# Last expert stage of a decoder: the small places of the second table mixed among the full ones

## The reference, cut to what matters

```python
h = silu(einsum('td,ehd->teh', xf, w1))          # 8 experts, 256 -> 512
expert_out = einsum('teh,edh->ted', h, w2)        # 512 -> 256
out = einsum('te,ted->td', comb, expert_out)      # comb is zero but for two experts of a token
x = x + out
```

## Time and profile before

| | us |
|---|---|
| median of 3 runs | 3156.68 |
| lowest and highest | 3152.07, 3157.47 |
| the profiled execution | 3149.4 |
| its span, first to last instruction | 3147.6 |
| mean granted clock of TensorE, share of full speed | 0.949 |

### The profile page before, as it was taken

One profiled execution on the slowest core, in us unless ns is written; L12 is line 12 of the kernel. 1 busy time (PEld: TensorE's weight loads), 2 busy tenths in 40 slices (PEclk: granted clock), 3 DMA queues, 4 the chain that ended last, 5 costly groups with the idle time before them and its releaser, 6 DMA issues.

```text
span 3147.6 us, 49455 instructions
## 1 busy us (share of the span) xinstructions
PE 2695.4 (86%) x16576; PEld 1841.3 (58%) x16576; DVE 1900.7 (60%) x3513; ACT 1524.2 (48%) x2641; POOL 1498.4 (48%) x1619
## 2 busy tenths in 40 slices
PE   5888888876888888878999999899888888868996
PEld 2333333323555566645688887697455555557885
DVE  3788888784787678863222222501688988883211
ACT  4565666543776666631122221444666666643332
POOL 3577666673545567634322222200345555543443
PEclk8999999988999999989999999899999999978998
DMA  9700000001005000002377775200000100006875
GB/s 326 240 0 1 0 1 1 1 0 38 20 16 189 1 1 0 1 22 89 104 217 207 210 211 156 71 1 1 1 16 31 37 33 31 22 20 193 231 216 155
DMA packets 137956, 244.75 MB, mean 78 GB/s; under 512 B 15936, under 2 KB 111424, under 8 KB 127040
## 3 DMA queue, kind: packets, MB, share of 16 engines
q1 hardware_dynamic: 111168, 207.61, 20.1%
q0 software_dynamic: 26592, 34.63, 5.6%
HBM read 151.28 MB, written 92.73 MB: 78 GB/s over the span
## 4 chain that ended last, share of the span: by engine, by line
PE 34%; DVE 6%; issue 6%; POOL 6%; ACT 2%; DMA 2%; POOLq 0%; DVEq 0%; ACTq 0%
PE PS L2442 11%; PE PS L2398 6%; PE PS L2066 4%; PE PS L2705 3%; PE PS L2718 3%; POOL e_hs L1544 3%; DMA out<-e_dead,f_token 2%; POOL e_qs L1547 1%; DVE e_mx L1447 1%; PE PS L1399 1%; POOL rows_in_place L878 1%; PE PS L2057 1%; DVE e_pr L1451 1%; PE PS L1337 1%; DVE e_den L1458 1%
## 5 line engine op out<-in xcount | busy, mean ns | idle before, releaser
L578 POOL TENSOR_TENSOR u_in<-dtx,b_rep 128x512 f32<-128x512 f32 x256 | 325.1, 1293 | 201.3 <-ACT b_rep L559 200.1
L594 DVE TENSOR_TENSOR_SCAN state<-PS,u_in 128x512 f32<-128x512 f32 x256 | 312.2, 1220 | 59.2 <-POOL u_in L578 34.9
L551 PE MATMUL PS<-scaled,ident 128*128 128x512 f32 x512 | 295.6, 661 | 28.8 <-DVE scaled L588 28.7
L2459 ACT ACTIVATE d_act_b<-PS 128x256 f32<-128x256 f32 (+2 forms) x192 | 76.6, 400 | 447.5 <-PE PS L2442 409.8
L1544 POOL TENSOR_TENSOR e_hs<-e_pr 128x512 f32<-128x512 f32 x128 | 162.9, 1272 | 236.5 <-ACT e_pr L1511 235.1
L1544 POOL TENSOR_TENSOR u_hs<-u_pr 128x512 f32<-128x512 f32 x128 | 166.1, 1298 | 229.1 <-ACT u_pr L1511 228.5
L2442 PE MATMUL PS<-d_unit_T,d_w 128*128 128x256 f32 (+1 forms) x1280 | 260.7, 356 | 1.1 <-ACT d_unit_T L2452 1.1
L2468 DVE TENSOR_TENSOR d_hid<-d_act_b,PS 128x256 f32<-128x256 f32 (+2 forms) x192 | 84.4, 440 | 283.3 <-ACT d_act_b L2459 246.1
L2362 POOL DMA_INDIRECT out_by_token<-d_y_rows,d_token x71 | 110.8, 1561 | 300.3 <-DVE d_y_rows L2489 201.6
L567 ACT ACTIVATE PS<-dt,decay_rate 128x508 f32<-128x508 f32 x256 | 173.5, 687 | 138.0 <-DVE state L594 136.1
L2442 PEld LDWEIGHTS PS<-d_unit_T,d_w 128*128 128x128 f32 x1280 | 221.0, 190 | 26.3 <-DVE d_hid L2468 1.3
(11 more groups left out here) (453 smaller groups left out, 6145.1 us busy)
## 6 DMA issues: line engine op xcount, KB each, us to landing
d_w<-in_d_w SPq DMA_DIRECT2D x42, 1024.0 KB, 6.1
e_dead<-in_f_w SPq DMA_DIRECT2D x40, 1024.0 KB
rows_in_place<-blank SPq DMA_DIRECT2D x136, 272.0 KB, 4.7
d_w<-in_d_w SPq DMA_DIRECT2D x42, 512.0 KB
rows_by_expert<-zeros SPq DMA_DIRECT2D x36, 272.0 KB, 3.6
d_unit_rows<-rows_by_expert SPq DMA_DIRECT2D x31, 272.0 KB
e_dead<-rows_in_place SPq DMA_DIRECT2D x31, 272.0 KB
X<-in_x SPq DMA_DIRECT2D x8, 512.0 KB, 11.7
```

What stands on the lines that cost most here:

```text
L551: nc.tensor.matmul(YB[:, c], ident[:], scaled[:, (KD * n + c) % RC], start=False, stop=n == NS - 1).then_inc(m_y, 1)
L578: nc.gpsimd.tensor_tensor(u_in[:, k % RU], dtx[:, p, c], b_rep[:, n % RB], ALU.mult).then_inc(m_u, 1)
L594: nc.vector.tensor_tensor_scan(state[:, k % 2], DECAY[:, k % RD], u_in[:, k % RU], 0.0, ALU.mult, ALU.add).then_inc(m_h, 1)
```

## The change

In the second table the places take another turn. After the 21 places of the first table come one full place, then nine times a full place and a small one. Before, ten full places came first and then nine small ones. The place numbers of each kind stay in their order, and the last place is the small one with the last number in both. Places 21 and 22 are the same as before; place 23 is now the first small one.

```diff
-    plan = [(2, 2 * n) for n in range(early)] + [(2, 2 * n) for n in range(full)]
-    return early, full, plan + [(1, 2 * full + n) for n in range(single)]
+    plan = [(2, 2 * n) for n in range(early)]
+    pairs, ones = [(2, 2 * n) for n in range(full)], [(1, 2 * full + n) for n in range(single)]
+    alone = max(full - single, 0)
+    plan += pairs[:alone]
+    for n in range(single):
+        plan += pairs[alone + n:alone + n + 1] + ones[n:n + 1]
+    return early, full, plan
```

## The result

The changed kernel is slower: its median is 3168.36 us of 18 runs (3158.98 to 3195.09), the kernel before has 3156.45 us in 18 runs beside it. The ratio is 1.0052 with a 95% interval from 1.0038 to 1.0065, so 12 to 21 us are lost. The forecast was 12 us gained.

What follows compares the result with a forecast made beforehand. The serial scatters bound the end: last output 3122.0, plus 0.14, 0.48 and 0.86, 3.4 lag and 8.7 to the end give span 3135.6, 12.0 us less; median 3156.7 to 3144.7 us, range 3138 to 3155.

Steps and rivals of the forecast that it cites:

- The chain of scatters bounds the end, not PE: End of the span: the last scatter is issued 13.6 us after PE's last output, so the serial scatters end last.
- PE's waits for weights go away, its last output comes 3 us earlier: Small places: three waits of 3.31 us in all taken as 0, PE's end from 3125.3 to 3122.0.
- the sum of the links: Second table: a link is the distance of two places' first scatters; a pair's two links keep pace up to 11.27 us.
- one slip: Nine pairs: only one has both links dear, 16.45 us, 5.2 over the cadence; lag at the last scatter taken as 3.4.
- the dear links (8.55 and 7.90): Profile before: link of full place 30 (8.55 us) and of a small place (7.90), used together for one pair.
- The argument for it was a share: Second table: a full and a small place take the DMA engines 9.1 of PE's 11.27 us, 0.81, leaving room.
- Four places now are 22.5 us of PE's time: DVE, token buffers: four places last 22.5 us and not 15.7, so its 12.7 us of waits for a buffer go.
- Rival 2: Full places' second tile waits behind the small place's weights: full links 8.55, small 5.16, loss 7.8 us; chance 0.08.
- a late chain thins the loads out: Argument against the slower case: a late chain lets PE run only four places ahead, and loads then thin out.
- The Trainium skill's rule on turns between queues: DMA engines: a tile waits behind one packet of a weight load, a full place's two tiles twice; speaks against the change.
- The last places win back 2 us: New places 37 to 39, empty with hardly a load: 9.0 us a pair against PE's 11.27, hiding 2 us of lag.
- The premise of the whole gain: Second table: with full and small places mixed the chain nearly keeps pace; 12.0 us gained, at most 15.4.

Runs made afterwards that it cites:

- e2: Changed kernel with eight token and y buffers, not four: first scatter of place 22 to that of place 39 115.1 us, ratio 1.0001 to the kernel before.
- e15: Changed order, eight token and y buffers, fourth weight buffer, wide POOL memset, but SP doesn't wait for it: places 22 to 39 115.9 us, ratio 1.0035 to before.
- e13: Changed order, eight token and y buffers, fourth weight buffer, loads wait for a wide POOL memset behind the scatters: places 22 to 39 98.2 us, ratio 0.9967 to before.
- e3: Changed kernel with each weight load issued as four of 256 KB: places 22 to 39 126.9 us, ratio 1.0095 to the kernel before.
- e4: Kernel before with each weight load issued as four of 256 KB: places 22 to 39 110.3 us, ratio 1.0031 to the kernel before.
- e1: Changed kernel, but places 24 to 39 load no weights: places 22 to 39 97.0 us, ratio 0.9958 to the kernel before.
- e6: Kernel before, but places 24 to 39 load no weights: places 22 to 39 98.0 us, ratio 0.9962 to the kernel before.
- e14: Kernel before with eight token and y buffers, fourth weight buffer, loads behind scatters by a wide POOL memset: places 22 to 39 99.6 us, ratio 0.9979 to before.
- e8: Changed kernel, eight token and y buffers, three weight buffers, loads wait for a narrow POOL memset behind the scatters: places 22 to 39 143.0 us, ratio 1.0112 to before.
- e10: Changed kernel, eight token and y buffers, four weight buffers, loads wait for a narrow POOL memset behind the scatters: places 22 to 39 107.7 us, ratio 1.0017 to before.
- e12: Changed kernel, but places 24 to 39 load only half the weights (512 KB): places 22 to 39 100.2 us, ratio 0.9960 to the kernel before.

## Why the prediction was wrong, point by point

- *The chain of scatters bounds the end, not PE:* right. Before and after it is what ended last, and all of the loss is in its links.
- *PE's waits for weights go away, its last output comes 3 us earlier:* wrong. Up to place 35 they did, and up to place 34 the loads came 7.0 and 4.5 us apart (7.0 and 4.3 forecast). Behind that PE waited 6.4 us. Counted from the scatter of place 22, its last output ended at 105.9 us and not at 95.3 as before. PE's four waits for weights all lie behind 3110 us, where the lock sets SP's beat, and in e2, without the lock, there is none. So this was a consequence of the late chain.
- *The step that failed is the sum of the links,* "I therefore don't add 1.3 us for each of nine pairs, 11.7 us, but count one slip ... 5.2 us over the cadence, and keeping pace before and after". The six pairs with loads took 97.3 us in place of 67.6: not one slip of 5 us but one in every pair. I had the dear links (8.55 and 7.90) in my rows and took them for exceptions. e15 against e13 shows that they are the rule in this order as long as loads go out in PE's beat. Among the full places of the order before, with one load in 7.35 us, they are not (links of 7.39 us in the mean).
- *The argument for it was a share:* 0.81 of the DMA engines' time being taken, there would be room. The share was 0.83 and didn't decide, as e13 runs a quick chain at 0.82. A serial chain pays for the moment at which it meets a load, and in the locked part it paid 7.3 to 9.6 us a link at a share of 0.58.
- *"Four places now are 22.5 us of PE's time", so DVE's waits for buffers go:* wrong, 53.3 us in place of 12.7. That would hold for a lag of 6 us; the chain was four places late from place 28 on. e2 puts 7.7 us of the stretch on this. In time the share is less certain: e2 recovers the whole loss (1.0001), e15, which has eight buffers and about the same stretch, only a third of it (1.0035).
- *Rival 2 was the right mechanism, and mis-sized:* it gave 8.55 for a full link and 5.16 for a small one, a loss of 7.8 us, with a chance of 0.08. Measured were 9.3 and 7.0, a loss of 13.9 us in the stretch. What I held against it, that a late chain thins the loads out and so helps itself, is the reverse of what happened: the thinned loads fell on the scatters one by one. Nor was it always the small place's weights that hit the second tile: the loads in the links of places 22, 28, 30 and 32 were a full place's.
- *The Trainium skill's rule on turns between queues* (DMA: Bandwidth & Descriptors, queues, rings and completion order), by which an engine drains a whole packet of one queue before it goes on to the next, had pointed the right way: full links were 9.3 us in the mean. But they weren't dear by a second load, as I had read it: only the links of places 22 and 26 had two (10.5 and 9.6 us), those of 28, 30 and 32 had one (9.6, 9.1 and 9.6). And e3 and e4, meant to test it with a packet taken to be one transfer's share (my assumption), made the engines busier, so no run here shows that the turn is what delays the scatters. The measured order of issue is what I rely on.
- *The last places win back 2 us:* right in kind. The five links that ended the stretch took 3.5 to 6.6 us, each less than PE's 7.0 and 4.5 for the place.
- *The premise of the whole gain* was that mixing is worth 12 to 15 us once nothing collides. e1 against e6 says 1 us, e13 against e14 1.4, neither more than single profiles can tell apart. What the order before loses to loads (108.9 against 98.0) goes away in e14 (99.6) without another order, with loads behind the scatters and a fourth weight buffer.

## What to carry to other kernels

Where a serial chain of transfers, each waiting for the last to land, shares the DMA engines with bulk loads, don't price it by the share of time that is free: look in the timeline at which load is issued just ahead of each of its transfers, and issue the loads behind them instead, with a buffer more where the later issue would make an engine wait (e8 against e13). Evening out the demand can be worse than a burst, if it puts a load beside every link. And follow a buffer's wait through the queues behind it: four token buffers, harmless while the chain was in time, tied the loads to the landings once it was late, and so kept it late.

## What the runs showed of the hardware

- With a weight load of 1 MB issued 0.33 us after the second tile's issue had ended, three full links were 9.5 to 10.7 us and three 7.1 to 7.4 (e10); with 1.2 to 1.5 us none was over 7.4 (e13).
- Half the load (512 KB) cost the chain 3.2 us over 16 loads, the whole one 25.8 (e12, changed, e1).
- The same weights in four transfers of 256 KB held the DMA engines for longer: a share of 0.99 and not 0.80 at 222 GB/s (e4, before). PE waited 15.0 and 13.3 us for weights, against 6.4 and 3.3 (e3, e4; changed, before).
- A memset of 128x1024 on POOL takes 1.55 us, and in e13 it lies in the time in which POOL waits for a landing anyway.
- An indirect DMA whose 128 rows are all out of bounds still takes 3.55 us from issue to the next issue, 1.0 us less than one with rows (before, places 37 and 34).
